# Second attention stage of a fused two-layer network: TensorE's value products in four runs of two key blocks instead of six runs

## The reference

```
x = x + _L1_attn_ref(_layernorm(x, axis=-1), L1_attn_Wq, L1_attn_Wk, L1_attn_Wv)

Q = (content @ Wq).reshape(b, n, HEADS, HEAD_DIM)
K = (content @ Wk).reshape(b, n, HEADS, HEAD_DIM)
V = (content @ Wv).reshape(b, n, HEADS, HEAD_DIM)
scores = jnp.einsum('bqhd,bkhd->bhqk', Q, K) / math.sqrt(HEAD_DIM)
alpha = jax.nn.softmax(scores, axis=-1)
alpha = jnp.where(causal, alpha, jnp.zeros((), dtype=alpha.dtype))
Y = jnp.einsum('bhqk,bkhd->bqhd', alpha, V).reshape(b, n, d)
```

## Time and profile before

| | |
|---|---|
| median of 3 runs | 1885.5 us (1883.88 to 1887.79) |
| the profiled execution, its own time | 1882.6 us |
| its span, first to last instruction | 1880.8 us |
| matmuls of the second attention stage (L1023, L1046) | 1115.6 to 1774.3 us of the span |
| one step of it, in the steady part | 9.96 us |

### The profile page before, as it was taken

The page is one execution under the profiler, slowest core; times in us unless marked ns, Lnnn a source line. Parts: engine busy times, 40 slices in busy tenths (PEclk is TensorE's granted clock), DMA queues, the critical chain, the costliest instruction groups (busy, mean ns, idle before and its releaser), DMA issues. The chain is left out here.

```text
span 1880.8 us, 48421 instructions
## 1 busy us (share of the span) xinstructions
PE 1642.7 (87%) x19050; PEld 1050.2 (56%) x19050; DVE 1562.8 (83%) x2531; ACT 1244.5 (66%) x2438; POOL 765.7 (41%) x1529
## 2 busy tenths in 40 slices
PE   5499999999554899999999638999999999999835
PEld 3277776767344687877667513444444444444424
DVE  7699999999397899998455669999999999999355
ACT  7388888888411444454333536889888988988725
POOL 3388888888661001000000123444444444444324
PEclk9699999999855999999999867999999999999958
DMA  8422222222250775754000261111111111111041
GB/s 267 161 83 86 88 85 86 87 84 82 74 116 11 98 94 91 92 90 71 1 1 0 91 211 41 56 53 55 59 55 53 58 57 54 54 59 47 19 101 45
DMA packets 131237, 141.87 MB, mean 75 GB/s; under 512 B 22797, under 2 KB 103882, under 8 KB 131018
## 3 DMA queue, kind: packets, MB, share of 16 engines
q1 hardware_dynamic: 130586, 138.79, 29.5%
q10 hardware_dynamic: 432, 0.07, 0.0%
HBM read 92.70 MB, written 44.98 MB: 73 GB/s over the span
## 5 line engine op out<-in xcount | busy, mean ns | idle before, releaser
L934 DVE TENSOR_REDUCE heads_mx<-heads_psM 128x1 f32<-128x1024 f32 x512 | 602.4, 1220 | 38.5 <-PE heads_psM L1023 22.6
L1003 ACT ACTIVATE heads_probs<-heads_psS 128x512 f32<-128x512 f32 x1024 | 546.0, 600 | 77.6 <-PE heads_psS L1046 71.7
L972 POOL TENSOR_TENSOR heads_masked<-heads_probs,g_tri 128x128 f32<-128x128 f32 x512 | 233.5, 456 | 361.0 <-ACT heads_probs L1003 360.9
L701 POOL TENSOR_TENSOR heads_probs<-heads_probs,one_ebias 128x256 f32<-128x256 f32 (+1 forms) x512 | 342.3, 695 | 76.3 <-ACT heads_probs L733 76.0
L733 ACT ACTIVATE heads_probs<-heads_psS 128x512 f32<-128x512 f32 x576 | 316.2, 602 | 60.9 <-PE heads_psS L744 55.6
L664 DVE TENSOR_REDUCE heads_mx<-heads_psM 128x1 f32<-128x1024 f32 (+7 forms) x512 | 349.4, 750 | 6.7 <-PE heads_psM L744 5.7
L1023 PE MATMUL heads_psM<-heads_kS,heads_qS 48*128 48x512 bf16 x1024 | 230.4, 395 | 27.3 <-DMA heads_kS<-k_parts 18.4
L1046 PE MATMUL heads_psS<-heads_qS,heads_kS 50*128 50x512 bf16 x1024 | 237.9, 389 | 0.7 <-ACT heads_probs L1003 0.3
L1528 ACT ACTIVATE trees_hid_hi<-trees_hid 128x512 fp32r<-128x512 f32 x192 | 121.7, 634 | 154.2 <-DVE trees_hid L1549 152.7
L1549 DVE SCALAR_TENSOR_TENSOR trees_hid<-trees_psH,g_b,trees_chosen 128x512 f32<-128x512 f32 x192 | 143.9, 750 | 34.5 <-DMA trees_chosen<-leaf_choice 17.5
L766 PE MATMUL heads_psM<-heads_kS,heads_qS 48*128 48x512 bf16 (+3 forms) x768 | 147.6, 334 | 21.8 <-DMA heads_kS<-k_parts 18.9
(11 more groups left out here) (252 smaller groups left out, 3189.6 us busy)
## 6 DMA issues: line engine op xcount, KB each, us to landing
heads_qS<-q_parts SPq DMA_DIRECT2D x256, 96.0 KB
heads_kS<-k_parts SPq DMA_DIRECT2D x256, 96.0 KB
trees_chosen<-leaf_choice SPq DMA_DIRECT2D x96, 256.0 KB
head_outputs<-heads_oT SPq DMA_DIRECT2D x128, 128.0 KB
heads_qS<-heads_mrow SPq DMA_DIRECT2D x256, 4.0 KB
q_parts<-open_parts SPq DMA_DIRECT2D x8, 384.0 KB, 3.5
k_parts<-open_parts SPq DMA_DIRECT2D x8, 384.0 KB, 4.3
q_parts<-proj_parts SPq DMA_DIRECT2D x8, 384.0 KB, 3.3
```

Of the source, the lines that this page charges most:

```text
L701: pool.tensor_tensor(pr[:, a:a + w], pr[:, a:a + w], bass.AP(eb.tensor, eb.offset + NEAR - 1, [list(eb.ap[0]), [-1, w]]), ALU.mult).then_i ...
L934: dve.tensor_reduce(mx[:, n % 2, k:k + 1], psM[k % 2][:, :], AXX, ALU.max, negate=True).then_inc(max_taken, 1)
L972: pool.tensor_tensor(masked[n % 2][:, kb, :], probs[n % 2][:, kb, kb * P:(kb + 1) * P], g["tri"][:, 0:P], ALU.mult).then_inc(near_done, 1)
L1003: act.activation(probs[n % 2][:, kb, h * CH:(h + 1) * CH], ring.bank(i)[:, :], ACT.Exp).then_inc(slot_taken, 1)
```

## The change

Only the order of PE's program in a step changes. The `values` are put into four runs, {0, 1}, {2, 3}, {4, 5}, {6, 7}. Between two runs stand two `scores`, one `maxima`, two `scores` and one `maxima`. The set of instructions is the same; so are the programs of the other engines, line by line.

```
@@ -1090,35 +1090,35 @@
                 scores(n, 0, 0)
                 scores(n, 0, 1)
                 maxima(n + 2, 2)
-                maxima(n + 2, 3)
                 scores(n, 1, 0)
                 scores(n, 1, 1)
+                maxima(n + 2, 3)
                 values(n - 1, 0)
                 values(n - 1, 1)
                 scores(n, 2, 0)
                 scores(n, 2, 1)
                 maxima(n + 2, 4)
-                values(n - 1, 2)
                 scores(n, 3, 0)
                 scores(n, 3, 1)
                 maxima(n + 2, 5)
+                values(n - 1, 2)
                 values(n - 1, 3)
                 rows(n + 1)
                 scores(n, 4, 0)
+                scores(n, 4, 1)
                 maxima(n + 2, 6)
-                scores(n, 4, 1)
                 scores(n, 5, 0)
+                scores(n, 5, 1)
+                maxima(n + 2, 7)
                 values(n - 1, 4)
-                maxima(n + 2, 7)
-                scores(n, 5, 1)
+                values(n - 1, 5)
                 scores(n, 6, 0)
+                scores(n, 6, 1)
                 maxima(n + 3, 0)
-                values(n - 1, 5)
-                values(n - 1, 6)
-                scores(n, 6, 1)
                 scores(n, 7, 0)
                 scores(n, 7, 1)
                 maxima(n + 3, 1)
+                values(n - 1, 6)
                 values(n - 1, 7)
```

## The result

| | before | after |
|---|---|---|
| median of 4 runs | 1886.16 us | 1964.61 us (1962.68 to 1966.57) |
| ratio, 95% interval | | 1.0417 [1.0399, 1.0435] |
| span of the profiled execution | 1880.8 us | 1960.9 us |
| one step of the second attention stage | 9.96 us | 11.23 us |

What follows compares the result with a forecast made beforehand. No engine was bound alone; PE's order set the 9.96 us step. Score stretches of 6.40 plus value stretches of 4.78 make 11.18 us; 1.22 more over 62.5 steps is 76 us: 1885.5 + 76 = 1962 us, range 1940 to 1980.

Steps and rivals of the forecast that it cites:

- The wait for the fourth score: Between two value runs on PE, the fourth score waits for a ring bank: 1.07 us behind the first.
- The stretch: On PE, from first score to next value run: 1.07 + 0.53 = 1.60 us, four a step making 6.40 us.
- rival 2: The wait holds only the score and PE fills it with the maxima: step 10.30 us, 1907 us; chance 6%.
- The value stretches: On PE, from a run's first value product to what follows: four sum to 4.78 us, 0.30 less than before.
- The sum: New step of the second attention stage: 6.40 + 4.78 = 11.18 us, 1.22 us more than 9.96.
- The count: Of the second attention stage's 64 steps, 62.5 counted as paying the loss: 76 us in all.
- Rival 1: PE sets the step and ring waits are hidden: 0.7 us a step less, 1842 us; chance 4%.
- Rival 3: PE's gaps in each stretch lower its clock to 1.2 GHz: some 240 us on top, 2200 us; chance 3%.
- The neighbours: GpSimd's triangles, `take_o`, `rows` and DMAs get more time and cost nothing; 0.05 us allowed if one ends late.
- VectorE's idle time: The added step time falls to VectorE as idle: 11.18 - 9.12 = 2.06 us a step.

Runs made afterwards that it cites:

- the parts: The change split in three, each alone on the kernel before: one maxima moved, 1898.4 us; runs {2} and {3} merged, 1907.8; the rest from `rows` on, 1923.5.
- e8: Order of the change, maxima over the first 512 keys only, ring of four banks, against the kernel before: 1824.7 us; timed again 1821.4 us, ratio 0.9656.
- e6: Order of the change, ring of three banks, against the kernel after with maxima over the first 512 keys only: 1931.2 us.

## Why the prediction was right

- **The wait for the fourth score**, 1.07 us from the first, in all four stretches. The trace after has 1.08 at both places shown and 1.07 or 1.08 in every stretch of the window. Shown as the cause from four sides: by the parts, by the maxima put into it, by the shorter exponential and by the fourth bank.
- **The stretch**, 1.60 us. Measured from the first score to the first value product: 1512.54 - 1510.92 = 1.62 us. That PE holds the maxima behind the waiting score is what keeps rival 2 out. The kernel with the maxima ahead of the fourth score shows about what rival 2 would have given: 1913 us, where the prediction said 1907.
- **The value stretches**, 1.25, 1.27, 1.03 and 1.23 us in the prediction. Measured: {0, 1} 1513.79 - 1512.54 = 1.25; {2, 3} with `rows` 1.27; {4, 5} 1519.31 - 1518.28 = 1.03; {6, 7} 1522.15 - 1520.92 = 1.23.
- **The sum**, 11.18 us a step. Measured 11.23. The four stretches are 1.62, 1.60 (1515.39 - 1513.79), 1.62 (1518.28 - 1516.66) and 1.61 us (1520.92 - 1519.31), together 6.45 where the sum had 6.40; that is the difference. The rows of the second half of the step:

```profile
1518.28 0.32 PE L1071 MATMUL heads_psO<-heads_probs,heads_ones_only 128*32 128x128 f32 x3
...
1519.31 0.39 PE L1046 MATMUL heads_psS<-heads_qS,heads_kS 50*128 50x512 bf16 x2
...
1520.92 0.30 PE L1071 MATMUL heads_psO<-heads_probs,heads_ones_only 128*32 128x128 f32 x1
...
1522.15 0.39 PE L1046 MATMUL heads_psS<-heads_qS,heads_kS 50*128 50x512 bf16 x2
```

- **The count.** From the first `rows` matmul to the last are 63 steps; they took 635.7 us before (1126.0 to 1761.7) and 711.7 after (1129.8 to 1841.5), 76.0 us more, which is the term of the prediction. That it fits so well is luck: at the measured 1.27 us a step, 62.5 steps would be 79 us. The steady steps do lose 1.27 us, but the first two distances lose nothing (15.12 and 12.32 us, where before they were 15.98 and 12.92), so a step that was put too short and a count that was put too high cancel. The spans differ by 80.1: another 3.8 us lie ahead of the first `rows`, where the two programs are the same. They are most of the 4.1 us between the 1958.6 us forecast for the profiled execution and its 1962.7.
- **Rival 1**, the hidden wait, needed the exponential to be over when PE comes to the fourth score. It isn't with three banks; with four it doesn't matter, and the gain appears (e8).
- **Rival 3**, the clock: 1.00 in the window of the stage. PE is busy 454.88 of 500 us, as far as records tell.
- **The neighbours** (`take_o`, GpSimd's triangles, `rows`, the DMAs) were costed at nothing. One wait on them is in the list: the third score behind `rows` waits for ScalarE's copy, 14.7 us in the window. It costs nothing in time, for that score starts 1517.11 - 1516.66 = 0.45 us behind the first, as in the stretch without `rows` (1511.37 - 1510.92).
- **VectorE's idle time**, 2.06 us a step in the prediction, is 80.6 / 44.5 = 1.81. The prediction took 1.14 us for each reduction, but now each pair comes by itself and takes 2.36. Nothing in the time hangs on it.

## What to carry to other kernels

Before you lengthen a run on one engine to save its changes of mode, count what then stands between two runs: if that needs more buffers than the ring has, each stretch costs one full round trip (here matmul, exponential and two hand-overs, 1.07 us), and the engine's order makes everything behind the waiting instruction pay as well. If such a wait can't be avoided, put work that needs no buffer ahead of it (0.22 us each here), and test the idea with one buffer more, even if work must be left out for it, before dropping it.

## What the runs showed that had not been expected

- With maxima over half the keys and three banks (e6), steps alternate between 10.37 and 11.23 us. The single maxima matmul uses rows 0 to 47, while scores change halves with each slot and a step has 17 slots, so from one step to the next it falls beside the fourth score or behind it. The fourth score comes 1.07 or 1.08 us behind the first in both kinds of step; what alternates is the piece from there to the run, 1502.35 - 1501.81 = 0.54 us at one step's start and 1512.93 - 1512.61 = 0.32 at the next one's. Four times 0.22 us is the difference between the two kinds. The explanation is read from the order of the slots and was not tried by itself.
- A stretch of PE with one gap of 0.25 us in every 2.8 shows as 91% busy (454.88 of 500), although PE starts nothing for 0.63 us between the third and the fourth score: the recorded length of a matmul, 0.38 us, covers the rest. The start-to-start distances told this, not the busy share.
